# Attention with two heads side by side in the array: 64-row products, shared PSUM areas, whole stacks in two transfers

## What is computed

```python
h = _layernorm(x) * (1 + ca) + sa
q, k, v = h @ Wq.T + bq, h @ Wk.T + bk, h @ Wv.T + bv   # 16 heads of 8
scores = einsum('bhqd,bhkd->bhqk', q, k) / sqrt(8)
attn = softmax(scores, axis=-1)
out = einsum('bhqk,bhkd->bhqd', attn, v)
x = x + ga * (out @ Wo.T + bo)
h = _layernorm(x) * (1 + cb) + sb
scores = h @ gate_w.T; topk = top_k(scores, 2); gating = softmax(topk)
x = x + gb * sum_e gating[e] * (silu(h @ wg[e].T) * (h @ wu[e].T)) @ wd[e].T
```

## Time and profile before

| | us |
|---|---|
| median of 3 runs | 1501.66 |
| lowest, highest | 1500.46, 1507.6 |
| profiled execution, its span | 1502.3 |

### The profile page before, as it was taken

The page is one execution under the profiler, slowest core; times in us unless marked ns, Lnnn a source line. Parts: engine busy times, 40 slices in busy tenths (PEclk is TensorE's granted clock), DMA queues, the critical chain, the costliest instruction groups (busy, mean ns, idle before and its releaser), DMA issues.

```text
span 1502.3 us, 26903 instructions
## 1 busy us (share of the span) xinstructions
PE 1191.8 (79%) x6826; PEld 567.9 (38%) x6827; DVE 1003.2 (67%) x2668; ACT 802.5 (53%) x1740; POOL 542.6 (36%) x595
## 2 busy tenths in 40 slices
PE   4285887979597879787978797879797989899982
PEld 2022322323232323232323232323232348798981
DVE  7294776959485859585958595868686845445556
ACT  3054665646465556555655564656564666455541
POOL 7020212324132324141415050505050347788764
PEclk9597988989898989898989898989898999999996
DMA  8220202121212121111212121202020132335677
GB/s 222 68 54 22 73 20 77 30 76 51 83 30 76 35 71 44 61 50 55 55 49 59 46 65 39 72 34 82 22 80 22 30 83 80 91 105 150 173 212 196
DMA packets 132900, 110.55 MB, mean 74 GB/s; under 512 B 22549, under 2 KB 123010, under 8 KB 129538
## 3 DMA queue, kind: packets, MB, share of 16 engines
q1 hardware_dynamic: 124082, 91.37, 22.0%
q0 software_dynamic: 8704, 17.97, 3.6%
HBM read 66.07 MB, written 41.18 MB: 71 GB/s over the span
## 4 chain that ended last, share of the span: by engine, by line
PE 52%; DMA 14%; SPq 13%; DVE 8%; issue 7%; POOL 3%; ACT 2%; DVEq 0%; ACTq 0%; POOLq 0%
PE ps L839 13%; PE ps L819 11%; PE ps L826 11%; DMA q_st<-shift_t 11%; DVE maxes L1324 4%; SPq L482 4%; PE ps L891 3%; PE ps L908 3%; PE ps L765 2%; SPq L500 2%; PE ps L900 1%; DMA k_st<-k_parts_d 1%; POOL ys_d L1575 1%; SPq L473 1%; PE ps L751 1%
## 5 line engine op out<-in xcount | busy, mean ns | idle before, releaser
L1324 DVE TENSOR_REDUCE maxes<-ps 128x1 f32<-128x512 f32 x1024 | 665.0, 681 | 284.1 <-PE ps L826 269.6
L1038 ACT ACTIVATE probs<-ps 128x512 f32<-128x512 f32 x1024 | 548.0, 606 | 231.2 <-PE ps L819 217.8
L819 PE MATMUL ps<-q_st,k_st 128*128 128x512 bf16 x1024 | 406.9, 400 | 176.2 <-DMA q_st<-shift_t 162.7
L826 PE MATMUL ps<-k_st,q_st 128*128 128x512 bf16 x1024 | 411.4, 403 | 59.9 <-DMA k_st<-k_parts_d 29.7
L1506 POOL TENSOR_TENSOR q_parts<-q,one 128x512 bf16<-128x512 f32 x16 | 16.6, 1035 | 752.0 <-ACT q L1013 752.0
L839 PE MATMUL ps<-probs,v_aug 128*32 128x512 f32 x2048 | 285.3, 631 | 1.1 <-ACT o_aug L1035 1.1
L819 PEld LDWEIGHTS ps<-q_st,k_st 128*128 128x128 bf16 x1024 | 105.2, 103 | 360.4 <-DMA q_st<-shift_t 174.3
L826 PEld LDWEIGHTS ps<-k_st,q_st 128*128 128x128 bf16 x1024 | 103.2, 101 | 202.0 <-DVE maxes L1324 97.2
L1536 POOL DMA_INDIRECT xs_d<-h,rows_o x128 | 123.8, 967 | 36.9 <-issue 36.5
L1447 DVE COPY probs<-ps 88x256 f32<-88x256 f32 x144 | 60.4, 420 | 98.0 <-PE ps L900 92.1
L908 PE MATMUL ps<-wd_t,probs 88*128 x576 | 93.7, 286 | 0.0
(11 more groups left out here) (203 smaller groups left out, 1356.9 us busy)
## 6 DMA issues: line engine op xcount, KB each, us to landing
k_st<-k_parts_d SPq DMA_DIRECT2D x96, 128.0 KB
q_st<-q_parts_d SPq DMA_DIRECT2D x128, 64.0 KB
q_parts_d<-q_parts SPq DMA_DIRECT2D x16, 384.0 KB, 2.9
k_parts_d<-k_parts SPq DMA_DIRECT2D x16, 384.0 KB
probs<-ys_d SPq DMA_DIRECT2D x24, 256.0 KB, 4.6
q_st<-xs_d SPq DMA_DIRECT2D x72, 65.0 KB
k_st<-xs_d SPq DMA_DIRECT2D x72, 65.0 KB
q_st<-q_parts_d SPq DMA_DIRECT2D x32, 128.0 KB
```

What stands on the lines that cost most here:

```text
L819: pe.matmul(ps[:, ST_BANK + bank, :], k_st[b % 2][:, j, P * t:P * (t + 1)], q_st[b % 2][side][:, j, :], start=True, stop=True).then_inc(st ...
L826: pe.matmul(ps[:, S_BANK + bank, :], q_st[bs % 2][side_s][:, js, P * t:P * (t + 1)], k_st[bs % 2][:, js, :], start=True, stop=True).then_i ...
L1038: act.activation(probs[:, g % 2, hh, S * t:S * (t + 1)], ps[:, ST_BANK + turn(QT * k + t)[0], :], ACT.Exp, scale=SCALE).then_inc(exps_done, 1)
L1324: dve.tensor_reduce(maxes[g % 2][:, hs % 2, hs // 2, t:t + 1], ps[:, S_BANK + bank, :], AX.X, ALU.max).then_inc(maxes_done, 1)
```

## The change

- `q_st` has one buffer a batch, both sides in it as in `k_st`. A product takes the rows of one half, 48 for looks and 50 for exps, and the products of an even and an odd head are issued one after the other, in the two halves of the array's rows.
- The two write neighbouring PSUM banks, an *area*. Three areas of two banks serve looks and exps in turn: a step makes one looks pair and one exps pair, a slot has two steps (four fills), and a fill waits for the reader of the area's last fill (`area_of`, `area_taken`).
- One maximum and one exp read both banks of an area.
- The six terms are stored to DRAM in the order of the stack, in three transfers each for q and k (twice the bytes), and loaded in two each. Shift rows take two transfers a group. The zero fills and their transfers at the start go.
- The expert map has SBUF of its own, and its token count goes through `misc`.
- ScalarE's copy of `o_aug` stands behind the slot's first (double) exp; h2T, score and where stand behind the slot's last fill.

```diff
-STACK_DMAS = 18
+STACK_DMAS = 4
+AREAS = 3
+STEPS = NH * QT // 2
+FILLS = 2 * STEPS
+def area_of(i):
+    return 1 if i == FILLS - 1 else i % AREAS
+def area_taken(b, i):
+    n, j = b, i
+    while n >= -2:
+        n, j = (n, j - 1) if j else (n - 1, FILLS - 1)
+        if area_of(j) != area_of(i):
+            continue
+        step, exps = n * STEPS + j // 2, j % 2
+        first = 0 if exps else -AHEAD_STEPS
+        if first <= step < NB * STEPS - (0 if exps else AHEAD_STEPS):
+            return exps, step - first + 1
+    return None, 0
...
-                for side in range(2):
-                    for part in range(2):
-                        row = SIDE * side + SHIFT + part
-                        src = 2 * QT * (2 * side + part)
-                        sp.dma_start(q_st[b % 2][side][row:row + 1, 2 * g:2 * g + 2, :],
-                                     shift_t[g % 2][src:src + 2 * QT, :]).then_inc(shift_stacked, 16)
+                for part in range(2):
+                    src = 4 * QT * part
+                    sp.dma_start(q_st[b % 2][SHIFT + part:SIDE + SHIFT + part + 1:SIDE, 2 * g:2 * g + 2, :],
+                                 shift_t[g % 2][src:src + 4 * QT, :]).then_inc(shift_stacked, 16)
...
+                for i, st, dram in ((0, q_st, q_parts_d), (1, k_st, k_parts_d)):
+                    wait(sp, parts_stored[i], lambda n: 48 * (n + 1), n, d)
+                    for side in range(2):
+                        lo = SIDE * side
+                        sp.dma_start(st[n % 2][lo:lo + SHIFT, :, :].rearrange("p j s -> p (j s)"),
+                                     dram[b][:, lo:lo + SIDE, :].rearrange("u (e j) s -> u e (j s)", e=DK)
+                                     ).then_inc(stack_ready, 16)
...
+                    for half in range(2):
+                        t, step = 2 * (hh % 2) + half, 2 * k + half
+                        if looks:
+                            if k == 8 and half == 0:
+                                wait(pe, stack_ready, lambda b: 16 * STACK_DMAS * (b + 2), b, d)
+                            free_area(b, 2 * step, d)
+                            for side in range(2):
+                                rows = slice(SIDE * side, SIDE * side + SHIFT)
+                                mm = pe.matmul(ps[:, 2 * area_of(2 * step) + side, :], q_st[bs % 2][rows, js, P * t:P * (t + 1)],
+                                               k_st[bs % 2][rows, js, :], start=True, stop=True)
+                            mm.then_inc(scores_ready, 1)
                         if exps:
-                            if hh == 0 and t == 0:
-                                wait(pe, shift_stacked, lambda b: 64 * (NG * b + g + 1), b, d)
...
+                            free_area(b, 2 * step + 1, d)
...
+                            act.activation(probs[:, g % 2, pair_at:pair_at + 2, S * t:S * (t + 1)],
+                                           ps[:, 2 * area:2 * area + 2, :], ACT.Exp, scale=SCALE).then_inc(exps_done, 1)
...
+                            dve.tensor_reduce(maxes[g % 2][:, :, hh // 2, tile:tile + 1], ps[:, 2 * area:2 * area + 2, :],
                                               AX.X, ALU.max).then_inc(maxes_done, 1)
```

More of the change, by code:

```diff
@@ L111, in batch_of @@
     return n if d is None else d * 2 + n
-def turn(i):
-    last = NH * QT - 1
-    before = i - TURN if i >= TURN else max(j for j in range(last + 1) if j % TURN == i % TURN) - last - 1
-    return i % TURN, i - before
+def area_of(i):
[11 more added lines that the diff above has]
+    return None, 0
 def along(eng, sem, f, q, d):
@@ L131, in misc_at @@
     s = NG * b + g
-    if not end:
+    if not end and (b, k) == COUNT_AT:
+        step = ("count", 0, 1)
+    elif not end:
         step = {4: ("h2T", b - 2, NB), 6: ("score", b - 2, NB), 13: ("where", b - 2, NB)}.get(k)
@@ L210, in adaln_block @@
         gtmp_r = probs[0:NB, 1, 2, HID:HID + 3 * D].rearrange("p (a d) -> p a d", d=D)
-        q_st = [[sb(f"q_st{i}_{side}", [P, PAIRS, S], BF16) for side in range(2)] for i in range(2)]
+        q_st = [sb(f"q_st{i}", [P, PAIRS, S], BF16) for i in range(2)]
         k_st = [sb(f"k_st{i}", [P, PAIRS, S], BF16) for i in range(2)]
@@ L278, in stack @@
             return st[:, :, :].rearrange("p j s -> p (j s)").bitcast(F32)
-        x_in = [stack((q_st[0][0], k_st[0])[i % 2])[:, XW * (i // 2):XW * (i // 2 + 1)] for i in range(SLOTS)]
-        part = parts(stack(q_st[0][1]))
+        x_in = [stack((q_st[0], k_st[0])[i % 2])[:, XW * (i // 2):XW * (i // 2 + 1)] for i in range(SLOTS)]
+        part = parts(map_area[:, :])
         tile_row = part(NPAIR * PADDED)[0:1].bitcast(I32).rearrange("p (q m) -> p q m", m=PADDED)
@@ L285, in adaln_block @@
         counts = part(NE)
+        count = part(NE)[0:1]
         needs = part(NE * FULL)[0:1].rearrange("p (e k) -> p e k", k=FULL)
@@ L292, in adaln_block @@
         start = part(TILES)[0:1]
-        y_last = y_last + [stack(q_st[1][i // 2])[:, 2 * S * (i % 2):2 * S * (i % 2 + 1)] for i in range(SBB - len(y_last))]
+        y_last = y_last + [stack((q_st[1], k_st[1])[i // 2])[:, 2 * S * (i % 2):2 * S * (i % 2 + 1)] for i in range(SBB - len(y_last))]
         gone = sb("gone", [P, 1])
@@ L782, in misc_step @@
                                        start=True, stop=True)
+                elif kind == "count":
+                    pe.wait_ge(map_step, 1)
+                    mm = pe.matmul(misc[0:1, 0:NE], ones[:, 0:1], counts, start=True, stop=True)
                 elif kind == "where":
@@ L803, in misc_steps, with free_area @@
                         misc_step(kind, n, 0, d)
+            def free_area(b, i, d):
+                exps, _ = area_taken(b, i)
+                if exps is not None:
+                    wait(pe, exps_done if exps else maxes_done, lambda b: area_taken(b, i)[1], b, d)
             def slot(b, k, d=None):
@@ new lines, in slot @@
+                    j, js, bs = 2 * g + hh // 2, (2 * g + hh // 2 + GROUP) % PAIRS, b + (g + 2) // NG
+                    for half in range(2):
[9 more added lines that the diff above has]
+                            mm.then_inc(scores_ready, 1)
+                        if exps:
+                            if hh == 0 and half == 0:
+                                wait(pe, shift_stacked, lambda b: 32 * (NG * b + g + 1), b, d)
+                            free_area(b, 2 * step + 1, d)
+                            for side in range(2):
+                                rows = slice(SIDE * side, SIDE * side + SHIFT + 2)
+                                mm = pe.matmul(ps[:, 2 * area_of(2 * step + 1) + side, :], k_st[b % 2][rows, j, P * t:P * (t + 1)],
+                                               q_st[b % 2][rows, j, :], start=True, stop=True)
+                            mm.then_inc(st_ready, 1)
+                        if half == 1:
@@ L868, in _ @@
                 batch(b)
-            for k in range(NH):
-                slot(NB - 1, k)
-                if k == MAP_AT:
-                    count_tokens(0, COUNT_BANK)
+            batch(NB - 1)
             for k in range(GROUP):
@@ L1486, in _ @@
             for i in range(2):
-                for side in range(2):
-                    pool.memset(q_st[i][side][SIDE * (1 - side):SIDE * (2 - side), :, :], 0.0).then_inc(zeros_ready, 1)
-                    pool.wait_ge(zeros_ready, 2 * i + side + 1)
-            for i in range(2):
                 pool.memset(v_aug[i][:, :, :, DK + 1:VW], 0.0).then_inc(fills_done, 1)
```

138 lines of the change are left out of this document (51 added, 87 removed).

## The result

| | before | after |
|---|---|---|
| median, us | 1503.24 (4 runs) | 1461.07 (4 runs) |
| lowest to highest | 1500.46 to 1507.6 | 1440.45 to 1471.91 |
| ratio | | 0.9641, 95% interval 0.9578 to 0.9703 |
| profiled execution, span | 1502.3 | 1463.7 |

The change makes the kernel faster: by 2.8% by the medians, by 3.6% by the ratio, which leaves out the runs counted as slow (over 1.5% above the fastest: 1465.6, which is the profiled one, and 1471.91). The forecast was 1420 us. The range holds the result; the likeliest value is 41 us too low. The profiled run took 1465.6 us at a mean clock of 0.879. The four runs spread more than those of before; the quickest has the highest clock (1440.45 us at 0.893), the longest the lowest (1471.91 at 0.867).

A forecast was written before the change was run, and what follows sets the result against it. The prediction took TensorE to bound the kernel, with 11% of the span a late shift-row transfer it waits for at slot k=8. Sum: 1502.3 - 161 - 35 - 18 + 124 + 9 - 1 = 1420 us; range 1368 to 1495.

The forecast's parts named there:

- The stall: TensorE's 16 waits for shift rows at slot k=8 go: 161 us gained, plus 35 from the slow clock behind them.
- rival 3: Stack loads still go over two DMA engines, so TensorE still waits at k=8: 1577 us, 6%.
- The start: Before the first maxima: without eight zero-fill transfers and with loads over 6 engines, 18 us gained.
- The chain through the first maximum: In each slot, looks pair, its maximum, exps pair, PV: 3.33 us against 2.82, +124 us over 244 slots.
- `d`: Time by which the second half of a product pair lags: taken as 0.10 us, between 0 and 0.216.
- rivals 1 and 2: Product pairs: halves run one after the other, 1476 us, 15%; a half's weight load isn't hidden, 1525 us, 10%.
- Cover that goes: VectorE and ScalarE steps now delay the chain, +36 us; 27 of TensorE's 97 us maximum waits go: net +9.
- Parts 2 and 3: The longer slots from areas of two banks, +124 us, and the lost cover for VectorE and ScalarE steps, +9.
- rival 4: The clock falls within slots since TensorE idles about 1 us in each: about +100 us, 1520 us, 4%.
- part 1: The stacks in 4 transfers a batch, shift rows in 2: stalls, slow clock and start, 161, 35 and 18 us gained.

The follow-up runs named there:

- e1: The kernel before with only the new stores and stack loads; banks, products and four shift-row transfers a group unchanged: 1353.07 us, ratio 0.8971.
- e10: e1 with stack rows in the order (e, u) and products on 48 or 50 rows in opposite halves, single banks kept: 1303.99 us, ratio 0.8657.
- e4: The kernel after with the second looks pair of a slot computed four times over, same values: 1397.73 us, ratio 0.9264 to the kernel before.
- e2: The kernel after with each stack load cut in three of two terms, 12 transfers a batch: 1658.98 us, ratio 1.0928 to the kernel before.
- e6: The same kernel as e10, run on another chip, where the kernel before took 1563.5 us: 1467.44 us, ratio 0.9366.
- e5: e1 with stack rows in the order (e, u), outermost count 8 for 6, on the chip of e6: 1464.03 us, ratio 0.9325.

## Why the prediction was right, and where it was off

**The stall went, and for the reason given.** 16 stalls with the clock behind them were put at 161 + 35 = 196 us; 174 us were measured in 15 batches, and batch 0 had one too. The share of the DMA engines was taken too high: 6/16 = 0.38 against 0.30 for the load alone, and the load took 18 us in the median batch where 9 to 15 were expected. The 0.50 for a count of 8 on which this rested was no measure of such loads: the stretch from 597 to 603 holds the store of the k parts, which keeps nearly all engines busy for over 1 us, and GpSimd's rows with 0.05. The rule itself, more engines with a larger outermost count, held, and rival 3 (two engines) fell. The margin at k=8 was thin enough that e1, with shorter slots and more shift-row transfers, still waits 44.5 us in all.

**The start** was put at 18 us. The first maximum came at 51.55 us in place of 68.83, 17.3 earlier:

```profile
51.55 9.15 DVE L1331 TENSOR_REDUCE maxes<-ps 128x2 f32<-128x1024 f32 x8 [15.00 <-PE ps L824]
```

**The chain through the first maximum** is there as drawn, and it hides the 0.86 us of product time that packing frees; e10, which packs without areas, collects part of it. The Trainium skill, "TensorEngine Tiling (Array Packing)", section "PSUM Bottleneck", says that packing speeds TensorE up and not the emptying of PSUM; this trace agrees, with TensorE idle for 0.89 us of a plain slot until a maximum is done. Two steps of the chain were taken too long, and they make up the whole error. `d` was 0.10, counted twice, and is 0, so rivals 1 and 2 fall. (The Trainium skill, "TensorE: Matmul & The Clock Gate", section "Part 3: Packing small matmuls — row/col tiling", puts the starts of such products about 4 ns apart; e10's trace agrees, with both at 644.09.) From the maximum's end to the exps pair 0.19 was taken, from a product that began 0.13 behind its weight load, and 0.05 measured (642.76 to 642.81). The rest was right: by the starts listed, looks pair to its maximum 0.42 taken and 0.43 measured (641.09 to 641.52), the maximum 1.21 and 1.24, exps pair to PV 0.31 and 0.32 (642.81 to 643.13). Slot 3.33 taken, 3.03 measured; +0.51 a plain slot taken, +0.21 measured.

**Cover that goes** was put at a net +9 us. At full clock a batch has 4.9 us more; the plain +0.21 in 16 slots explains 3.4, and 1.5 a batch, 23 us, is left for it. It is in the slots with steps in them: k=5 went from 4.12 to 4.77, k=13 from 3.31 to 3.84. Parts 2 and 3 together were put at +133 us and came to +74.

**The clock is the step that failed.** The sum had no term for it. It was rival 4, with 4% and +100 us, and its sign, a low clock away from the loop's ends, is there (0.57 from 646 to 656 us). It cost 81 us over the 15 batches of the profiled execution, and e4, with useless work in the idle time, took some 65 of them back, which shows the mechanism. The profiled span is 44 us above the sum. The slots account for -59 (133 taken, 74 measured), the clock for +81, the stalls and batch 0 for +16, the tail for +4, 42 together. So the right answer was a shorter chain and rival 4 at once, and two errors partly cancelled.

**That the range holds the result is in part luck.** It reached above 1461 by its room for slower slots, `d` up to a whole product, and none of that came. With the slots as measured and no clock term the sum would have been 1361, below the range's lower end of 1368; that end took `d` = 0 and left next to nothing for the other terms. The direction was not luck, since the stall and the start outweighed all the rest.

The evidence against the rival was one stretch of 6 us before attention, where the clock was still 1.00 with TensorE half idle. Another stretch of that length says the opposite: from 79 to 85 us, at another place of the program, the kernel after has a clock of 0.57 with TensorE busy for 5.46 of 6 us (columns as in the earlier trace rows):

```profile
79.00:85.00 6.00, 5.46 (x26) 2.53 (x28) 4.32 (x6) 4.01 (x6) 0.00 (x0) 0.57 0.62 185
```

A short stretch tells what the clock was, and not what it will be in 240 slots that idle in the same way. The plain stretches of the earlier trace rows at 1.00 belonged to slots without idle time.

## What to carry over

Before you give two readers a shared buffer, draw the loop through it: product, reader, next product that needs the buffer, and whatever stands behind that in the same queue. A faster engine that then waits once in every loop may lose its clock as well, and that loss was here as large as the longer loop itself; price it from how the slots at the lower level read, and try part of the change alone, since part 1 without the areas was worth 10% and with them 3.6%. A small transfer behind large ones waits for them (the shift rows took 10 us to land before, 12.86 in e1), so count how many DMA engines the large one's outermost dimension can reach. And before you read a share of the DMA engines as that of one transfer, take out what other queues moved in the same stretch.

## What the runs showed of the hardware

- Filling idle TensorE time with repeated products made the kernel after 4.3% faster by the medians (e4 1397.7, after 1461.1), the granted clock of attention going from 0.87 to 0.97.
- The share of the 16 DMA engines that a stack load takes goes with its outermost count: 0.14 for 2 (e2), 0.30 for 6 (after), 0.42 for 8 (e10). The load of a batch took 30.2, 18 and 14.1 us.
- Two products of 48 to 50 rows in opposite halves of the array start in the same hundredth of a microsecond, whether issued as a pair with one wait (after) or as two kinds with their own waits, where neither has to wait (e10).
- A maximum over two banks takes 1.219 us in the mean, against 0.681 for one bank, and 9.15/8 = 1.14 in an unbroken run, against 0.604: joining two saves 5 to 10%.
- One chip ran all kernels slower, the kernel before by 3.8%, in pauses of all three compute engines near rows of scatters. A ranking that was made there (e5 and e6 equal) turned into 3.5% for e6's kernel over e1's on an undisturbed one (e5's did not run there). Why that chip pauses is open.
